# Graph-transformer kernel: in the edge pass VectorE weighs the value rows and sums the key products two quads at a time

## The chip, the cores and the metric

The kernel runs on one core of one Trainium2 chip. The time is the device time of one execution in microseconds; lower is better.

## The reference, cut to what matters

The program is a two-layer graph transformer over 3125 nodes with 256 features and 100,000 edges sorted by destination. What the change touches is the edge attention of the second layer (8 heads of 32 columns):

```python
scores = jnp.einsum('ehd,ehd->eh', q[dst], k[src] + ep[:, None, :]) * scale
scores = scores * ew[:, None]
m = jax.ops.segment_max(scores, dst, num_segments=n)
ex = jnp.exp(scores - m[dst])
s = jax.ops.segment_sum(ex, dst, num_segments=n)
attn = ex / s[dst]
out = jax.ops.segment_sum(attn[:, :, None] * v[src], dst, num_segments=n)
```

Everything is float32.

## The kernel before, in words

`stage_flash` is the edge pass. Edges are taken in sub-blocks of 128, one edge on each partition. 16 sub-blocks are a *window*, four sub-blocks a *quad* (`G` = 4 quads in a window). There are `NW` = 52 windows. For each sub-block GpSimd gathers 128 rows of 520 columns into a slot of a ring in SBUF: the key's 256 columns (`LO`) and 264 value columns (`HI_`, 33 a head, of which the last is a one that gives the sum of the weights). The ring has two sides of 16 slots.

Each engine runs the loop `windows`, whose `body(s, a, ffn)` does two windows at once: window `s` gets its scores, window `a`, the one before, is weighed and added up. The first call has only `s`, the last only `a`, 51 have both; 50 of these have `ffn` too, half a tile of another layer's feed-forward on TensorE and ScalarE.

For window `s`, quad by quad:

- TensorE, `ask(s, g)`: eight matmul instructions in the trace fetch the query rows of the quad's edges into `query`, a PSUM tile that holds one quad. It waits for `mult(s, g - 1)`, which frees that tile, and for the selection matrix `mem_t` from ScalarE.
- VectorE, `add(s, g)` (L2701): key rows plus edge features. `mult(s, g)` (L2708): times `query`, after `ask(s, g)`. `reduce(s, g)` (L2712): the sum over a head's 32 columns, into `dots`. After four quads `scale(s)` (L2718) makes the scores of the window.

For window `a`: TensorE transposes the scores (L2528), VectorE makes running maxima (`within`, `across`, `lower`) with small matmuls between them, ScalarE makes the exponentials `pa` (L2645). Then:

- VectorE, `rescale(a)` (L2768) on the row of `acc` that is carried on, and `weigh(a, g)` (L2773): the quad's value rows times their weights, which raises `pv_ready` by 1.
- TensorE, `collect(a, n)` (L2513) for sub-block pairs n = 0 to 7: sums of the value rows by destination. It waits for `pv_ready` of its quad, n // 2. `fold(a, n)` (L2520) adds the accumulator; ScalarE's `keep` (L2623) copies the sum back. A fold frees ring slots for GpSimd's next gathers.

Each engine works its queue strictly in the order of `body`; the order was written by hand. On TensorE it is: transpose of the scores, feed-forward, small matmuls, `ask(s, 0)`, small matmuls, feed-forward, `ask(s, 1)`, collects and folds of pairs 0 to 2, `ask(s, 2)`, pairs 3 and 4, `ask(s, 3)`, the rest. Semaphores count: `pv_ready` rises by `G` = 4 a window, and so do `mult_done` and `reduce_done`.

Of the kernel before, what the change touches and what calls it, by code (L numbers as in the profile page):

```python
# [18 lines left out]
ALU = mybir.AluOpType  # L19
# [3 lines left out]
P = 128  # L23
# [11 lines left out]
WS = 16  # L35
# [2271 lines left out]
def stage_flash(nc, sh, w1, w2, b1):  # L2307
# [6 lines left out]
    with ExitStack() as ctx:  # L2314
# [107 lines left out]
        with nc.Block() as block:  # L2422
# [246 lines left out]
            def _(dve):  # L2669
# [23 lines left out]
                def key_rows(s, g):  # L2693
                    return ring[:, s.side * WS + 4 * g:s.side * WS + 4 * g + 4, LO]
# [12 lines left out]
                    r = key_rows(s, g)  # L2707
                    dve.tensor_tensor(r, r, query[:, :].rearrange("p (k f) -> p k f", k=4), ALU.mult).then_inc(mult_done, 1)  # L2708

                def reduce(s, g):  # L2710
                    dve.wait_ge(mult_done, G * s.at + (g + 1))
                    dve.tensor_reduce(dots[:, g * 4 * H:(g + 1) * 4 * H].rearrange("p (k h) -> p k h", h=H),  # L2712
                                      key_rows(s, g).rearrange("p k (h d) -> p k h d", h=H), AX.X, ALU.add
                                      ).then_inc(reduce_done, 1)

                def scale(s):
                    dve.wait_ge(reduce_done, G * s.at + G)
# [49 lines left out]
                    r = sh.acc[:, bass.ds(tile, 1), :, :].rearrange("p a h v -> p (a h) v")  # L2767
                    dve.tensor_tensor(r, r, pa[:, P:P + H].unsqueeze(2).to_broadcast([P, H, VW]), ALU.mult).then_inc(rescaled, 1)  # L2768

                def weigh(a, g):  # L2770
                    r = ring[:, a.side * WS + 4 * g:a.side * WS + 4 * g + 4, HI_].rearrange("p k (h v) -> p k h v", h=H)
                    e = pa[:, 0:P].rearrange("p (h j) -> p j h", h=H)[:, 4 * g:4 * g + 4, :]
                    dve.tensor_tensor(r, r, e.unsqueeze(3).to_broadcast([P, 4, H, VW]), ALU.mult).then_inc(pv_ready, 1)  # L2773

                def body(s, a, ffn):
                    if a is not None and s is not None:
                        dve.tensor_copy(index[:, a.side * WS:(a.side + 1) * WS], sh.src_of[:, bass.ds(WS * s.at + WS, WS)]
                                        ).then_inc(index_ready, 1)
                    if s is not None:
                        add(s, 0)  # L2780
                    if a is not None:
                        within(a)
                        across(a)
                    if s is not None:
                        add(s, 1)
                    if a is not None:
                        lower(a)
                    if s is not None:
                        mult(s, 0)
                    if a is not None:  # L2790
                        tile = dve.value_load(sh.tile_id[0:1, bass.ds(WI * a.at, 1)], min_val=0, max_val=NT - 1)
                        rescale(a, tile)
                        weigh(a, 0)
                        weigh(a, 1)
                    if s is not None:
                        mult(s, 1)
                        add(s, 2)
                    if a is not None:
                        weigh(a, 2)
                    if s is not None:  # L2800
                        reduce(s, 0)
                        reduce(s, 1)
                        mult(s, 2)
                    if a is not None:
                        weigh(a, 3)
                    if s is not None:
                        add(s, 3)
                        reduce(s, 2)
                        mult(s, 3)
                        reduce(s, 3)  # L2810
                        scale(s)
                    if ffn is not None and ffn[1] == 1:
                        i = ffn[0]
                        dve.wait_ge(down_ready, 2 * i + 3)
                        w = sh.work[:, bass.ds(i, 1), :].rearrange("p a f -> p (a f)")
                        dve.tensor_tensor(w, w, down[:, 0:D], ALU.add).then_inc(down_added, 1)
# [415 lines left out]
```

## Time and profile before

| | |
|---|---|
| median of 3 runs | 4058.91 us (4058.58 to 4063.38) |
| span of the profiled execution, first to last instruction | 4057.2 us |
| VectorE busy | 2274.9 us (56%) |
| TensorE matmul busy | 3096.2 us (76%) |
| GpSimd busy | 1908.2 us (47%) |
| edge pass, from about 2215 to 3550 us of the span | about 1335 us |

The profile gives no other time of that execution than its span; the median of the runs is 1.7 us above it. In the views that follow, a row of the order of time is: start in us, duration in us (from the first start to the last end, where several are merged), engine, line, operation, what it writes and reads, count, and in brackets the idle time before it with what ended it. The end of one VectorE instruction can lie behind the start of the next, since the next one starts before the last results are written.

### The profile page before, as it was taken

The numbers are of one execution on the slowest core, as the hardware profiler recorded it, in microseconds if no ns is written. First come the engines' busy times: TensorE is split into PE (matmuls) and PEld (weight loads), VectorE is DVE, ScalarE is ACT, GpSimd is POOL, SyncE is SP. The second block draws the span as 40 slices with busy tenths as digits, with TensorE's granted clock in tenths as the row PEclk, the third lists the DMA queues.
The fourth block names the chain that finished last, engine by engine and source line by source line (L and its number), as shares of the span: only waits on it lengthen the run. The fifth ranks groups of instructions, "written<-read, shape, count | busy, mean of one in ns | idle before, by whom it ended". The sixth has DMA issues, their size and how long they took to land. (4 is left out here: it accounts for less than half of the span.)

```text
span 4057.2 us, 61852 instructions
## 1 busy us (share of the span) xinstructions
PE 3096.2 (76%) x13267; PEld 2402.7 (59%) x13268; DVE 2274.9 (56%) x5192; ACT 1703.0 (42%) x3865; POOL 1908.2 (47%) x1849
## 2 busy tenths in 40 slices
PE   2587777777767639906753899999999999849888
PEld 1476666666653438803332677777777777636655
DVE  6243333333345300043475899999999999762524
ACT  1333333333332112301402677777777777622413
POOL 2477777777760130040013666666666666420010
PEclk9677777778778569957876999999999999969999
DMA  5555555555540046623002777777777777510000
GB/s 145 160 150 144 145 143 142 143 143 144 143 97 0 14 141 205 204 67 123 32 0 90 223 217 215 216 216 216 213 215 217 218 217 217 157 39 22 1 24 32
DMA packets 347067, 552.91 MB, mean 136 GB/s; under 512 B 169831, under 2 KB 230771, under 8 KB 343109
## 3 DMA queue, kind: packets, MB, share of 16 engines
q0 software_dynamic: 114432, 353.45, 30.7%
q1 hardware_dynamic: 232305, 197.83, 17.0%
q10 hardware_dynamic: 260, 0.80, 0.1%
q8 instruction: 31, 0.51, 0.1%
q14 instruction: 39, 0.32, 0.0%
HBM read 489.26 MB, written 63.83 MB: 136 GB/s over the span
## 5 line engine op out<-in xcount | busy, mean ns | idle before, releaser
L2475 POOL DMA_INDIRECT store<-kv_d,flash_index x832 | 891.8, 1072 | 403.9 <-issue 227.9
L814 POOL DMA_INDIRECT agg_rows<-xn_d,agg_index x832 | 791.6, 951 | 321.9 <-issue 226.6
L839 ACT ACTIVATE agg_rows<-agg_rows,weight_of 128x256 f32<-128x256 f32 x832 | 368.5, 499 | 605.2 <-DMA agg_rows<-xn_d,agg_index 603.0
L989 PE MATMUL agg_sums<-agg_rows,agg_member 128*128 128x257 f32 x1664 | 515.5, 477 | 125.8 <-DVE agg_member L918 125.8
L989 PEld LDWEIGHTS agg_sums<-agg_rows,agg_member 128*128 128x128 f32 x1664 | 400.0, 247 | 223.3 <-ACT agg_rows L839 76.2
L925 DVE TENSOR_TENSOR acc<-acc,agg_sums 128x257 f32 x416 | 176.5, 424 | 589.6 <-PE agg_sums L989 507.3
L2500 PE MATMUL flash_query<-q,flash_mem_t 128*128 x1664 | 411.9, 391 | 50.6 <-DVE store L2708 38.7
L2513 PE MATMUL flash_sums<-store,flash_member 128*128 128x264 f32 x1664 | 423.0, 387 | 2.2 <-DVE store L2773 2.2
L2500 PEld LDWEIGHTS flash_query<-q,flash_mem_t 128*128 128x128 f32 x1664 | 313.2, 193 | 103.7 <-issue 63.1
L981 PE MATMUL agg_edge<-agg_we,agg_feats 65*128 65x32 f32 x1664 | 276.3, 336 | 114.0 <-DMA agg_feats<-in_ef_t_dram 113.9
L981 PEld LDWEIGHTS agg_edge<-agg_we,agg_feats 65*128 65x128 f32 x1664 | 271.9, 259 | 131.1 <-issue 130.3
L2513 PEld LDWEIGHTS flash_sums<-store,flash_member 128*128 128x128 f32 x1664 | 314.1, 191 | 59.2 <-issue 2.4
L2708 DVE TENSOR_TENSOR store<-store,flash_query 128x1024 f32<-128x1024 f32 x208 | 252.9, 1216 | 27.8 <-PE flash_query L2500 27.8
L2614 ACT ACTIVATE flash_member<-lane,lane_of 128x128 f32<-128x128 f32 x832 | 264.7, 395 | 0.0
L2520 PE MATMUL flash_sums<-acc,ident 128*128 x832 | 259.2, 393 | 1.5 <-ACT acc L2623 1.5
L2701 DVE TENSOR_TENSOR store<-store,flash_ep 128x1024 f32<-128x1024 f32 x208 | 253.1, 1217 | 8.9 <-DMA flash_ep<-ep_d 8.9
L2773 DVE TENSOR_TENSOR store<-store,flash_pa 128x1056 f32<-128x1056 f32 x208 | 256.1, 1253 | 0.0
L2623 ACT ACTIVATE acc<-flash_sums 128x264 f32 x416 | 159.3, 383 | 229.3 <-PE flash_sums L2520 222.8
L2712 DVE TENSOR_REDUCE flash_dots<-store 128x32 f32<-128x1024 f32 x208 | 248.3, 1216 | 1.8
L918 DVE TENSOR_SCALAR agg_member<-lane,lane_of 128x128 f32<-128x128 f32 x832 | 177.4, 303 | 34.8 <-issue 34.8
L1563 DVE COPY expert_y<-expert_down 128x512 f32<-128x512 f32 x32 | 22.1, 692 | 298.8 <-PE expert_down L1530 298.8
L2520 PEld LDWEIGHTS flash_sums<-acc,ident 128*128 128x128 f32 x832 | 145.6, 190 | 46.0 <-issue 30.6
(440 smaller groups left out, 4627.5 us busy)
## 6 DMA issues: line engine op xcount, KB each, us to landing
expert_w<-in_L_ffn_W_dram SPq DMA_DIRECT2D x64, 512.0 KB, 4.5
agg_feats<-in_ef_t_dram SPq DMA_DIRECT2D x52, 512.0 KB
flash_goal<-goal_d SPq DMA_DIRECT2D x52, 512.0 KB, 4.3
agg_rows<-xn_d,agg_index POOLq DMA_INDIRECT x832, 2.7
ep_d<-agg_ep SPq DMA_DIRECT2D x52, 256.0 KB
store<-kv_d,flash_index POOLq DMA_INDIRECT x832, 4.0
flash_ep<-ep_d SPq DMA_DIRECT2D x416, 32.0 KB
flash_flags<-flags_d SPq DMA_DIRECT2D x416, 32.0 KB
```

The costliest lines, as they stand in the source:

```text
L814: pool.indirect_dma_start(rows[:, q, 0:D], None, sh.xn_d, bass.IndirectOffsetOnAxis(ap=index[:, q:q + 1], axis=0)).then_inc(gathered[u], 16)
L839: act.activation(rows[:, q, 0:D], rows[:, q, 0:D], ACT.Copy, scale=sh.weight_of[:, bass.ds((UI * i + u) * SUBS + k, 1)]).then_inc(weighted, 1)
L981: last = pe.matmul(edge[:, c * DH:(c + 1) * DH], feats[:, c * P:(c + 1) * P], we_s[:, :], start=True, stop=True)
L989: last = pe.matmul(sums[:, u % 4, 0:W], member[:, u % WI * SUBS + k, :], rows[:, q, :], start=(k == 0), stop=(k == SUBS - 1))
L2475: pool.indirect_dma_start(ring[:, s, :], None, sh.kv_d, bass.IndirectOffsetOnAxis(ap=index[:, s:s + 1], axis=0)).then_inc(gathered[p][g], 16)
L2500: last = pe.matmul(query[:, c * D:(c + 1) * D], mem_t[:, g % 2, c * P:(c + 1) * P], sh.q[:, bass.ds(t, 1), :], start=True, stop=True)
L2513: pe.matmul(sums[:, n % 3, 0:W], member[:, g % 2, c, :], ring[:, a.side * WS + 4 * g + c, HI_], start=(k == 0), stop=False)
L2520: pe.matmul(sums[:, n % 3, 0:W], sh.ident[:, :], sh.acc[:, bass.ds(tiles[n], 1), :, :].rearrange("p a h v -> p (a h v)"), start=False, sto ...
L2614: act.activation(member[:, g % 2, k, :], sh.lane[:, :], ACT.Abs, scale=-1.0, bias=sh.lane_of[:, bass.ds(WS * a.at + (4 * g + k), 1)])
L2701: dve.tensor_tensor(r, r, ep[:, s.side, 4 * g:4 * g + 4, :].unsqueeze(2).to_broadcast([P, 4, H, DH]), ALU.add).then_inc(add_done, 1)
L2708: dve.tensor_tensor(r, r, query[:, :].rearrange("p (k f) -> p k f", k=4), ALU.mult).then_inc(mult_done, 1)
L2773: dve.tensor_tensor(r, r, e.unsqueeze(3).to_broadcast([P, 4, H, VW]), ALU.mult).then_inc(pv_ready, 1)
```

## The change

`weigh(a, g)` is replaced by `weigh_two(a, g)`: one instruction over 8 slots, which raises `pv_ready` by 2. `reduce(s, g)` is replaced by `reduce_two(s, g)`: one instruction over 8 slots, which waits for the `mult` of both quads and raises `reduce_done` by 2. `body` calls them in the order below.

```diff
-                def reduce(s, g):
-                    dve.wait_ge(mult_done, G * s.at + (g + 1))
-                    dve.tensor_reduce(dots[:, g * 4 * H:(g + 1) * 4 * H].rearrange("p (k h) -> p k h", h=H),
-                                      key_rows(s, g).rearrange("p k (h d) -> p k h d", h=H), AX.X, ALU.add
-                                      ).then_inc(reduce_done, 1)
+                def reduce_two(s, g):
+                    dve.wait_ge(mult_done, G * s.at + (g + 2))
+                    r = ring[:, s.side * WS + 4 * g:s.side * WS + 4 * g + 8, LO]
+                    dve.tensor_reduce(dots[:, g * 4 * H:(g + 2) * 4 * H].rearrange("p (k h) -> p k h", h=H),
+                                      r.rearrange("p k (h d) -> p k h d", h=H), AX.X, ALU.add).then_inc(reduce_done, 2)
...
-                def weigh(a, g):
-                    r = ring[:, a.side * WS + 4 * g:a.side * WS + 4 * g + 4, HI_].rearrange("p k (h v) -> p k h v", h=H)
-                    e = pa[:, 0:P].rearrange("p (h j) -> p j h", h=H)[:, 4 * g:4 * g + 4, :]
-                    dve.tensor_tensor(r, r, e.unsqueeze(3).to_broadcast([P, 4, H, VW]), ALU.mult).then_inc(pv_ready, 1)
+                def weigh_two(a, g):
+                    r = ring[:, a.side * WS + 4 * g:a.side * WS + 4 * g + 8, HI_].rearrange("p k (h v) -> p k h v", h=H)
+                    e = pa[:, 0:P].rearrange("p (h j) -> p j h", h=H)[:, 4 * g:4 * g + 8, :]
+                    dve.tensor_tensor(r, r, e.unsqueeze(3).to_broadcast([P, 8, H, VW]), ALU.mult).then_inc(pv_ready, 2)
...
                         rescale(a, tile)
-                        weigh(a, 0)
-                        weigh(a, 1)
+                        weigh_two(a, 0)
                     if s is not None:
                         mult(s, 1)
                         add(s, 2)
                     if a is not None:
-                        weigh(a, 2)
+                        weigh_two(a, 2)
                     if s is not None:
-                        reduce(s, 0)
-                        reduce(s, 1)
+                        reduce_two(s, 0)
                         mult(s, 2)
-                    if a is not None:
-                        weigh(a, 3)
-                    if s is not None:
                         add(s, 3)
-                        reduce(s, 2)
                         mult(s, 3)
-                        reduce(s, 3)
+                        reduce_two(s, 2)
                         scale(s)
```

VectorE's queue in the loop body, from the rescale of `acc` to the instruction before `mult(s, 2)` (L2708 is `mult`, L2701 `add`, L2773 `weigh` or `weigh_two`, L2712 `reduce`, L2713 `reduce_two`; `-` is before, `+` is now):

```order
 L2768 TENSOR_TENSOR acc<-acc,flash_pa 128x264
-L2773 TENSOR_TENSOR store<-store,flash_pa 128x4x264 x2
+L2773 TENSOR_TENSOR store<-store,flash_pa 128x8x264
 L2705 REGISTER_ALU
 L2708 TENSOR_TENSOR store<-store,flash_query 128x4x256
 L2701 TENSOR_TENSOR store<-store,flash_ep 128x4x256
-L2773 TENSOR_TENSOR store<-store,flash_pa 128x4x264
-L2712 TENSOR_REDUCE flash_dots<-store 128x32 x2
+L2773 TENSOR_TENSOR store<-store,flash_pa 128x8x264
+L2713 TENSOR_REDUCE flash_dots<-store 128x64
```

The first two quads are weighed by one instruction, and quad 3 has moved up in front of the sums of the key products.

The same queue from `mult(s, 2)` to `scale(s)`:

```order
 L2705 REGISTER_ALU
 L2708 TENSOR_TENSOR store<-store,flash_query 128x4x256
-L2773 TENSOR_TENSOR store<-store,flash_pa 128x4x264
-L2701 TENSOR_TENSOR store<-store,flash_ep 128x4x256
-L2712 TENSOR_REDUCE flash_dots<-store 128x32
+L2701 TENSOR_TENSOR store<-store,flash_ep 128x4x256
 L2705 REGISTER_ALU
 L2708 TENSOR_TENSOR store<-store,flash_query 128x4x256
-L2712 TENSOR_REDUCE flash_dots<-store 128x32
+L2713 TENSOR_REDUCE flash_dots<-store 128x64
 L2718 ISA
 L2718 SCALAR_TENSOR_TENSOR flash_scaled<-flash_dots,weight_of 128x16x8
```

Between `mult(s, 2)` and `mult(s, 3)` only `add(s, 3)` is left; the sum of quad 2 has moved behind `mult(s, 3)`. The queues of the other engines are the same as before.

## Rows read from the trace of the kernel before

**Rows 1.** The page: span, busy time of each engine, VectorE in 40 slices.
```profile
span 4057.2 us, 61852 instructions
...
PE 3096.2 (76%) x13267; PEld 2402.7 (59%) x13268; DVE 2274.9 (56%) x5192; ACT 1703.0 (42%) x3865; POOL 1908.2 (47%) x1849
...
DVE  6243333333345300043475899999999999762524
```
**Rows 2.** Stretches: length, busy PE, PEld, DVE, ACT, POOL (instructions); granted clock, DMA, GB/s.
```profile
2602.34:2627.00 24.66, 23.03 (x111) 18.69 (x111) 22.98 (x37) 18.09 (x42) 16.91 (x17) 1.00 0.74 212
2627.00:2652.13 25.13, 23.72 (x115) 19.23 (x115) 23.31 (x38) 17.50 (x42) 17.39 (x17) 1.00 0.76 221
```
**Rows 3.** Order of time on VectorE (DVE), one window from `mult(s, 0)` to `scale`.
```profile
2609.38 1.21 DVE L2708 TENSOR_TENSOR store<-store,flash_query 128x1024 f32<-128x1024 f32 x1
...
2611.07 2.42 DVE L2773 TENSOR_TENSOR store<-store,flash_pa 128x1056 f32<-128x1056 f32 x2
2613.41 1.22 DVE L2708 TENSOR_TENSOR store<-store,flash_query 128x1024 f32<-128x1024 f32 x1
...
2615.67 1.25 DVE L2773 TENSOR_TENSOR store<-store,flash_pa 128x1056 f32<-128x1056 f32 x1
2616.84 2.34 DVE L2712 TENSOR_REDUCE flash_dots<-store 128x32 f32<-128x1024 f32 x2
2619.59 1.22 DVE L2708 TENSOR_TENSOR store<-store,flash_query 128x1024 f32<-128x1024 f32 x1 [0.41 <-PE flash_query L2500]
...
2623.04 1.22 DVE L2712 TENSOR_REDUCE flash_dots<-store 128x32 f32<-128x1024 f32 x1
2624.16 1.21 DVE L2708 TENSOR_TENSOR store<-store,flash_query 128x1024 f32<-128x1024 f32 x1
2625.41 1.22 DVE L2712 TENSOR_REDUCE flash_dots<-store 128x32 f32<-128x1024 f32 x1
2626.78 0.37 DVE L2718 SCALAR_TENSOR_TENSOR flash_scaled<-flash_dots,weight_of 128x128 f32<-128x128 f32 x1
```
**Rows 4.** Order of time on TensorE (PE) in the same window.
```profile
2610.84 1.99 PE L2500 MATMUL flash_query<-q,flash_mem_t 128*128 x8 [0.68 <-DVE store L2708]
2612.67 1.05 PE L2513 MATMUL flash_sums<-store,flash_member 128*128 128x264 f32 x4
...
2617.60 1.89 PE L2500 MATMUL flash_query<-q,flash_mem_t 128*128 x8
...
2621.99 1.89 PE L2500 MATMUL flash_query<-q,flash_mem_t 128*128 x8
...
2626.42 0.64 PE L2520 MATMUL flash_sums<-acc,ident 128*128 x2
2627.21 0.33 PE L2528 MATMUL flash_small<-ident,flash_scaled 128*128 128x128 f32 x1
```
**Rows 5.** Order of time in the last window, which has only `a`.
```profile
3533.96 4.76 DVE L2773 TENSOR_TENSOR store<-store,flash_pa 128x1056 f32<-128x1056 f32 x4
...
3535.31 2.10 PE L2513 MATMUL flash_sums<-store,flash_member 128*128 128x264 f32 x4 [2.17 <-DVE store L2773]
```
**Rows 6.** Groups by form on VectorE, 2200 to 3400 us: busy, mean ns, idle before.
```profile
L2773 DVE TENSOR_TENSOR store<-store,flash_pa 128x1056 f32<-128x1056 f32 x184 | 226.7, 1253 | 0.0
...
L2768 DVE TENSOR_TENSOR acc<-acc,flash_pa 128x264 f32 x46 | 20.0, 434 | 5.6
```
**Rows 7.** Waits of VectorE in 36 windows (2602.34 to 3498.8): total, times, longest.
```profile
DVE store L2708 <- PE flash_query L2500: 14.9, 36, 0.4
```
**Rows 8.** Order of time on TensorE in the window without feed-forward, and that stretch.
```profile
3501.40 0.23 PE L2544 MATMUL flash_small<-flash_z,flash_row_head 128*8 128x32 f32 x2 [2.40 <-DVE flash_z L2733]
3501.61 3.67 PE L2500 MATMUL flash_query<-q,flash_mem_t 128*128 x8
...
3498.80:3526.20 27.40, 22.55 (x87) 17.63 (x88) 22.79 (x37) 14.45 (x35) 9.67 (x9) 0.88 0.37 99
```
**Rows 9.** Order of time on GpSimd (POOL): the first gather behind a wait.
```profile
2616.33 1.42 POOL L2475 DMA_INDIRECT store<-kv_d,flash_index  x1 [3.18 <-PE flash_sums L2520]
```

## Prediction

> **What bounds the kernel now.** I read the busy shares first. The edge pass is the stretch of slices in which VectorE's digit is 9: the pass keeps VectorE at nine tenths and more, while over the whole span it is busy for little over half [rows 1]. A window of 16 ring slots takes 24.66 and 25.13 us in turn; of these VectorE is busy 23.0 to 23.3 us and TensorE 23.0 to 23.7 us [rows 2]. Two engines at 93 to 95% can't be told apart by their shares, so I read the two engines' order of time inside one window, from `mult(s, 0)` at 2609.38 to `scale` at 2626.78, which is 17.40 us [rows 3, 4].
>
> In that stretch each engine waits for the other once. TensorE starts `ask(s, 1)` at 2610.84 after waiting 0.68 us for `mult(s, 0)` [rows 4]. From there on it runs one row behind the other: eight query matmuls, the `collect` and `fold` pairs, `ask(s, 2)` at 2617.60, more pairs, `ask(s, 3)` at 2621.99. VectorE waits 0.41 us for `ask(s, 2)`, and starts `mult(s, 2)` at 2619.59, 1.99 us behind that ask's start [rows 3, 4]. This isn't one odd window: in 36 windows VectorE's wait for the query comes 36 times and none is above 0.4 us, 14.9 us in all [rows 7]. So from `mult(s, 0)` to `mult(s, 2)` the path runs through TensorE, and from `mult(s, 2)` to `scale` through VectorE, which does seven instructions there without a gap. From `scale` to the next `mult(s, 0)` (24.9 - 17.4 = 7.5 us on average) VectorE is on the path again; the change touches nothing there.
>
> GpSimd isn't the bound: it waits 3.18 us for a `fold` that frees ring slots, and starts to gather at 2616.33 what VectorE adds to behind the next `scale` [rows 9]. A later `fold` delays the gathers by less than the window grows, below, so this cover stays.
>
> **What is in hand at mult(s, 3).** It starts at 2624.16, right behind `reduce(s, 2)` [rows 3]. By the 1.99 us just read, `ask(s, 3)`, which starts at 2621.99, would have let it start at 2623.98. So the slack of TensorE's path is only 0.18 us at this point, and what VectorE does between `mult(s, 2)` and `mult(s, 3)` was hidden time for TensorE almost to the last tenth.
>
> **The change, part by part.** Per window, four `weigh` become two of double size and four `reduce` become two.
>
> *Price of a double instruction.* A `weigh` of 1056 elements takes 1253 ns, the rescale (the same kind of operation) of 264 elements 434 ns [rows 6]: 819 / 792 = 1.034 ns an element. The second half of a double `weigh` adds 1056 x 1.034 = 1.09 us; of a double `reduce`, 1024 x 1.034 = 1.06, up to the 1.13 us that lies between starts of 1024-element instructions that don't depend on each other (two of them fill 2613.41 to 2615.67) [rows 3]. I take 1.07. The instruction saved is worth start distance less streaming time: 1.17 - 1.09 = 0.08 us for a `weigh`, 1.13 - 1.07 = 0.06 for a `reduce`, so 2 x 0.08 + 2 x 0.06 = 0.28 us of VectorE's work a window.
>
> *Step 1, the first collect.* `collect(a, 0)` needs quad 0 alone, but its semaphore now moves when quads 0 and 1 are both weighed. Before, quad 0 was ready at 2611.07 + 1.25 = 2612.32, hidden behind `ask(s, 1)`; the collect started at 2612.67 when TensorE came free. Now both are ready at 2611.07 + 1.25 + 1.09 = 2613.41. How fast TensorE follows is seen where it did wait for a `weigh`: the last window, the first of four starts at 3533.96 and ends 1.25 us later, at 3535.21, and TensorE starts at 3535.31, 0.10 us [rows 5]. The nearest rows on both sides are 0.06 us (`scale`'s end, 2627.15, to the transpose at 2627.21) and 0.25 us (`mult(s, 0)`'s end, 2610.59, to the ask at 2610.84) [rows 3, 4]. I take 0.10: the collect starts at 2613.51, 0.84 us late (0.80 to 0.99). Behind it stand the whole of TensorE's queue: all collects and folds, `ask(s, 2)`, `ask(s, 3)`. ScalarE's copies of the sums wait for the folds and move along with them. TensorE has no gap until `ask(s, 3)` in which to catch up [rows 4], so all of it is 0.84 us late.
>
> *Step 2, quad 3 weighed earlier.* `weigh_two(a, 2)` puts 1.09 us more in front of `mult(s, 2)`. VectorE would have been ready for that at 2619.18; now at about 2619.18 + 1.09 - 0.14 = 2620.1. The query comes at 2619.59 + 0.84 = 2620.43. Hidden by step 1's delay; without step 1 it would cost about 0.5 us at `mult(s, 2)`, though not at `mult(s, 3)`, since there is 1.17 us less behind it.
>
> *Step 3, what stood between mult(s, 2) and mult(s, 3).* `weigh(a, 3)` and `reduce(s, 2)` are gone from there, `add(s, 3)` alone is left. That can't bring `mult(s, 3)` forward, since its query isn't there: `ask(s, 3)` starts at 2621.99 + 0.84 and lets it start at 2624.82, 0.66 us later than before. VectorE is ready at about 2620.43 + 1.13 + 1.25 = 2622.8 and stands idle for 2.0 us.
>
> *Step 4, the last reduce.* Behind `mult(s, 3)` there was one quad to sum, now there are two: +1.07 us (1.06 to 1.13) until `scale`. `reduce(s, 2)`, which ran in time that TensorE needed anyway, now runs in time that everybody waits for: the transpose at 2627.21 begins right behind `scale` [rows 3, 4], and the whole chain to the next `mult(s, 0)` hangs on it.
>
> The sum for a window: 0.84 - 0.18 + 1.07 = 1.73 us; by the bounds 0.80 - 0.18 + 1.06 = 1.68 to 0.99 - 0.18 + 1.13 = 1.94. Windows that do both halves of the work: 51. The first window (scores only) has step 4 alone, +1.07; the last (weighing only) step 1 alone, +1.09. Together 51 x 1.73 + 2.2 = 90 us, with bounds of 88 and 101. The span becomes 4057.2 + 90.4 = 4147.6 us; the median of the runs is 1.7 us above the profiled span, so 4149 us, with 4147 to 4160 from the bounds.
>
> The 0.28 us of saved work is all inside the 2.0 us of new idle time, so it is worth nothing. The Trainium skill ("VectorE: DVE Perf Modes", the section on the TRN2 errata, and "Rules for kernel authors") says the opposite of this forecast: every SBUF instruction pays a fixed latency once, so few large ones are better, and one should minimize the number of operations. The trace agrees on the fixed cost (0.06 to 0.08 us an instruction) but not on its being on the path.
>
> **The rivals.**
> *The count decides (faster).* VectorE is the bound at 93%, so less work is less time: -0.28 x 51 = -14 us, 4045 us. For it speaks only the busy share. It needs TensorE to be off the path between `mult(s, 0)` and `mult(s, 3)`: it would decide if TensorE's stretch from 2610.84 to 2623.98 were shorter by over 1.7 us (0.84 + 1.07 - 0.18), which the 0.41 us wait excludes.
> *The shifts cancel (no change).* TensorE's late start is absorbed by its own waits elsewhere and the moved `weigh` gives `mult(s, 3)` what step 4 takes: 4059 us. Against it stands the 0.18 us.
> *One delay alone.* TensorE makes up its late start before `ask(s, 3)`, because its ends are modelled and it isn't as full as it seems. Then step 4 stays: 1.07 - 0.18 = 0.89 a window, 51 x 0.89 + 2 = 47 us, 4106 us.
> *TensorE's clock falls (slower still).* TensorE now idles about 0.7 us before the first collect (2610.84 + 1.99 = 2612.83 to 2613.51) and about 1 us before the transpose (the last fold ends at 2626.42 + 0.64 + 0.84 = 2627.90, `scale` at 2627.15 + 1.73), and 1.6 + 1.7 = 3.3 us of a 26.6 us window in all [rows 2, 4]. In the last full window, which has no feed-forward matmuls, it waited 2.40 us and its next eight query matmuls took 3.67 us in place of 1.89 to 1.99: the granted clock had gone to the lower level, 1.2 GHz [rows 8]. That window took 27.4 us (3498.80 to 3526.20), 2.6 more than a usual one. If every window did so, 51 x 2.6 = 133 us on top: about 4280 us. Against it: the new idle stretches are each shorter than 2.40 us, with 2 us of matmuls between them.
>
> **How the numbers follow.** Forecast 0.77; one delay alone 0.10; clock 0.05; cancel 0.04; count 0.04. The forecast's own range is 4142 to 4164 us (the bounds, and 4 us either way for what the windows differ by). That leaves 0.23 out, so the range goes down to the single delay: 4104 to 4164. A change of 0.2%, 8 us, is about what can be told from none. Faster 0.04, the same 0.04, slower 0.92.
>
> **What would show it.** Right: a full window of 26.4 to 26.8 us; VectorE waiting for the query some 2.0 us before `mult(s, 3)` and 0.3 us before `mult(s, 2)`; TensorE waiting for the double `weigh` before the first collect, once a window; double instructions of 2.28 to 2.35 us; the transpose about 19.5 us behind `mult(s, 0)` in place of 17.8; TensorE's clock at full. Wrong: the first collect still behind the ask at once (step 1), `mult(s, 3)` at the old distance of 14.8 us from `mult(s, 0)` (step 3), a double instruction priced other than 1.07 to 1.13 us above a single one (step 4), query matmuls of over 3 us per ask (clock), or a window of under 24.7 us (count).

## The result: 110 us slower, and the profile after

On the same chip, with four runs of each, the changed kernel takes 4169.81 us (4161.95 to 4173.39) and the kernel before 4059.57 us (4058.58 to 4063.38). The ratio is 1.0267, 95% interval 1.0252 to 1.0281: slower. The forecast was 4149 us with a range up to 4164: the time lies 6 us above the range. Direction and mechanism held, and the size of the loss was forecast too small.

The page of after: span, busy time of each engine, VectorE in 40 slices.

```profile
span 4160.3 us, 61748 instructions
...
PE 3107.1 (75%) x13267; PEld 2398.4 (58%) x13268; DVE 2267.8 (55%) x4984; ACT 1705.8 (41%) x3865; POOL 1871.2 (45%) x1849
...
DVE  5243333333445200143576888888888888862524
```

VectorE issues 208 instructions fewer (5192 to 4984, four in each of 52 windows) and is busy 7.1 us less, while the span is 103.1 us longer [rows 1]. Its digit in the edge pass fell from 9 to 8: the engine that looked like the bound now has idle time.

Two groups by form on VectorE, 2200 to 3500 us (busy, mean ns of one, idle before), answer to [rows 6]:

```profile
L2773 DVE TENSOR_TENSOR store<-store,flash_pa 128x2112 f32<-128x2112 f32 x92 | 216.3, 2351 | 0.0
L2713 DVE TENSOR_REDUCE flash_dots<-store 128x64 f32<-128x2048 f32 x94 | 214.5, 2282 | 4.8
```

A double `weigh` is 2351 - 1253 = 1098 ns above a single one. The price of a double instruction was right (1.09 forecast, and 2.28 to 2.35 us for the whole).

The waits of after between 2200 and 3560 us (total, times, longest) answer to [rows 7]:

```profile
DVE store L2708 <- PE flash_query L2500: 130.2, 98, 3.9
...
PE flash_sums L2513 <- DVE store L2773: 40.5, 49, 0.8
```

Before, VectorE waited for the query once a window, 0.4 us each. Now it waits twice a window, 98 times, and TensorE has a wait that it didn't have: 0.83 us for the double `weigh`, once a window.

Order of time on VectorE in one window of after, from `mult(s, 0)` to `scale`; it answers to [rows 3]:

```profile
2608.47 1.22 DVE L2708 TENSOR_TENSOR store<-store,flash_query 128x1024 f32<-128x1024 f32 x1
...
2610.15 2.35 DVE L2773 TENSOR_TENSOR store<-store,flash_pa 128x2112 f32<-128x2112 f32 x1
...
2619.77 1.22 DVE L2708 TENSOR_TENSOR store<-store,flash_query 128x1024 f32<-128x1024 f32 x1 [0.54 <-PE flash_query L2500]
2620.91 1.22 DVE L2701 TENSOR_TENSOR store<-store,flash_ep 128x1024 f32<-128x1024 f32 x1
2624.17 1.22 DVE L2708 TENSOR_TENSOR store<-store,flash_query 128x1024 f32<-128x1024 f32 x1 [2.04 <-PE flash_query L2500]
2625.49 2.29 DVE L2713 TENSOR_REDUCE flash_dots<-store 128x64 f32<-128x2048 f32 x1
2627.92 0.38 DVE L2718 SCALAR_TENSOR_TENSOR flash_scaled<-flash_dots,weight_of 128x128 f32<-128x128 f32 x1
```

And on TensorE in the same window; it answers to [rows 4]:

```profile
2609.93 1.99 PE L2500 MATMUL flash_query<-q,flash_mem_t 128*128 x8 [0.68 <-DVE store L2708]
2612.74 1.15 PE L2513 MATMUL flash_sums<-store,flash_member 128*128 128x264 f32 x4 [0.83 <-DVE store L2773]
2613.73 0.61 PE L2520 MATMUL flash_sums<-acc,ident 128*128 x2
...
2617.78 1.89 PE L2500 MATMUL flash_query<-q,flash_mem_t 128*128 x8
...
2622.17 1.89 PE L2500 MATMUL flash_query<-q,flash_mem_t 128*128 x8
...
2628.36 0.33 PE L2528 MATMUL flash_small<-ident,flash_scaled 128*128 128x128 f32 x1 [1.11 <-DVE flash_scaled L2718]
```

To compare the two kernels I measure every instruction from `mult(s, 0)` of its window. Medians over the 51 full windows, in us:

| behind `mult(s, 0)` | before | after |
|---|---|---|
| first `collect` | 3.29 | 4.27 |
| `mult(s, 2)` | 10.21 | 11.31 |
| `ask(s, 3)` | 12.61 | 13.70 |
| `mult(s, 3)` | 14.79 | 15.70 |
| `scale(s)` | 17.40 | 19.46 |
| from `scale` to the next `mult(s, 0)` | 7.8 | 7.8 |

(The rows of `collect` and `ask(s, 3)` are from the windows shown in [rows 3, 4] and above.) Nearly all the loss lies between `mult(s, 0)` and `scale`: 2.06 us. Over the pass, the first `scale` to the 52nd goes from 2251.8 to 3526.2 us before and from 2248.9 to 3629.8 after: 24.99 and 27.08 us a window, 51 x 2.09 = 106.5 us. Outside this stretch the span is 3.4 us shorter, which gives the 103.1. The profiled run was the shortest of the four of after; the medians differ by 110.

### The profile page after: what moved, and what is told of

Its sections match the earlier page's. It is cut to its first block and busy times, and to the rows that moved or that the text cites. A ratio compares the mean times of both kernels' runs of the same rounds, so it can differ in the third digit from the quotient of the medians.

```text
span 4160.3 us, 61748 instructions
## 1 busy us (share of the span) xinstructions
PE 3107.1 (75%) x13267; PEld 2398.4 (58%) x13268; DVE 2267.8 (55%) x4984; ACT 1705.8 (41%) x3865; POOL 1871.2 (45%) x1849
## 5 line engine op out<-in xcount | busy, mean ns | idle before, releaser
L2475 POOL DMA_INDIRECT store<-kv_d,flash_index x832 | 854.8, 1027 | 545.3 <-PE flash_sums L2520 302.6
L2708 DVE TENSOR_TENSOR store<-store,flash_query 128x1024 f32<-128x1024 f32 x208 | 253.2, 1217 | 138.4 <-PE flash_query L2500 138.4
L2701 DVE TENSOR_TENSOR store<-store,flash_ep 128x1024 f32<-128x1024 f32 x208 | 253.7, 1220 | 9.2 <-DMA flash_ep<-ep_d 8.2
L2773 DVE TENSOR_TENSOR store<-store,flash_pa 128x2112 f32<-128x2112 f32 x104 | 244.4, 2351 | 0.0
L2713 DVE TENSOR_REDUCE flash_dots<-store 128x64 f32<-128x2048 f32 x104 | 237.3, 2282 | 5.4
```

The costliest lines, as they stand in the source:

```text
L2475: pool.indirect_dma_start(ring[:, s, :], None, sh.kv_d, bass.IndirectOffsetOnAxis(ap=index[:, s:s + 1], axis=0)).then_inc(gathered[p][g], 16)
L2701: dve.tensor_tensor(r, r, ep[:, s.side, 4 * g:4 * g + 4, :].unsqueeze(2).to_broadcast([P, 4, H, DH]), ALU.add).then_inc(add_done, 1)
L2773: dve.tensor_tensor(r, r, e.unsqueeze(3).to_broadcast([P, 8, H, VW]), ALU.mult).then_inc(pv_ready, 2)
```

## The experiments

**How they are read.** The runs `v0` and `v5` were on a chip on which the kernel before takes 4060 us, as in the result. All others were on five other chips, on which the kernel before takes 4777 to 4828 us. I call these the slow chips. On them every kernel has additional stalls, in the edge pass and before it. In the views of waits, `remote` is a release by something that isn't an instruction of this core's profile, and `issue` is time in which the engine waited for nothing that the profile shows. The waits of the kernel before on such a chip, between 2500 and 3560 us:

```profile
ACT acc L2623 <- remote: 198.1, 50, 6.7
PEld flash_sums L2520 <- issue: 171.5, 90, 5.9
...
DVE store L2708 <- remote: 58.3, 23, 9.6
```

A window takes 33.8 us there in place of 25.0. The durations of instructions at full clock are the same, and some windows have no stall between `mult(s, 0)` and `scale`: I call them undisturbed. In the list of distances of all 51 windows they are the shortest. There are one to eleven of them in each run, only one in `z0`, `x2`, `y2`, `w7`, `u1` and `u3`; within a kernel they agree to 0.05 us. So on these chips the order of time inside undisturbed windows tests the theory, and the total only tells what a kernel does amid the stalls.

TensorE's clock is lower there too. Between 2600 and 4200 us the granted clock (the number ahead of the DMA share, columns as in [rows 2]) is 0.89 for the kernel before (`z0`), 0.89 for the changed one (`z5`) and 0.86 for one that comes below (`z3`), where the pass on the fast chip has 1.00:

```profile
2600.00:4200.00 1600.00, 1245.74 (x5293) 999.21 (x5293) 1104.02 (x1723) 841.34 (x1955) 773.37 (x759) 0.89 0.56 159
...
2600.00:4200.00 1600.00, 1223.02 (x5181) 972.38 (x5181) 1071.08 (x1499) 825.08 (x1920) 759.46 (x743) 0.89 0.55 156
...
2600.00:4200.00 1600.00, 1224.26 (x5110) 970.31 (x5111) 1059.50 (x1577) 816.33 (x1903) 812.39 (x731) 0.86 0.55 153
```

**The kernels of the result again.** `z0` is the kernel before and `z5` the changed one, unaltered, on one slow chip.

> The kernel before, unchanged, for its trace. If this chip is like that of the x and y runs: some 4780 us and, once a window, a stall of 4 to 6 us on all engines that no semaphore explains, as in x1 to x4, so that the stalls belong to the chip and not to the experiments. If the stalls come with the edits: 4059 us and none of them.

> The changed kernel, unchanged, beside the kernel before on this chip. Where VectorE isn't disturbed, scale 19.46 us behind mult(s, 0). On a chip without the stalls +108 us, a ratio of 1.027. On a chip with them the ratio is smaller if the stalls cover part of the two delays, and 1.022 (108 / 4780) if they only add.

Measured: `z0` 4789.53 us beside 4787.62 in the other runs of before; its undisturbed window has `mult(s, 3)` at 14.79 and `scale` at 17.40. `z5` 4830.48 us, ratio 1.0084 (1.0056 to 1.0113); four undisturbed windows with 15.70 and 19.45. Both patterns are those of the fast chip to 0.01 us, so the reading by undisturbed windows holds. The price in total is about a third of that on the fast chip: the time from `scale` to the next `mult(s, 0)`, summed over the 50 gaps between full windows, is 697 us for `z0` and 652 for `z5` (377 and 380 on the fast chip). So the gain there, 45 us, takes back part of what the longer windows cost; I read it as stalls that were there anyway and that the later `scale` covers.

**Undo step 1** (the steps are those of the prediction; step 1 is the first collect). The changed kernel with the first double `weigh` as two single ones:

```diff
-                        weigh_two(a, 0)
+                        weigh(a, 0)
+                        weigh(a, 1)
```

> The changed kernel with its first double weigh split again into weigh(a, 0) and weigh(a, 1); the double reduces and the double weigh of quads 2 and 3 stay. Two delays in series: the first collect is no longer late (2.05 less 1.10 us a window), mult(s, 3) comes 0.18 us earlier than in the kernel before, and the doubled last reduce costs 1.13, so +0.95 us a window over before, about 4059 + 49 = 4108 us. If the long reduce alone made the loss: no gain over the changed kernel, 4168. If the late collect alone made it: 4059.

Order of time on VectorE in an undisturbed window:

```profile
3146.33 1.22 DVE L2708 TENSOR_TENSOR store<-store,flash_query 128x1024 f32<-128x1024 f32 x1
...
3148.01 2.42 DVE L2773 TENSOR_TENSOR store<-store,flash_pa 128x1056 f32<-128x1056 f32 x2
...
3160.94 1.22 DVE L2708 TENSOR_TENSOR store<-store,flash_query 128x1024 f32<-128x1024 f32 x1 [1.51 <-PE flash_query L2500]
...
3164.70 0.37 DVE L2718 SCALAR_TENSOR_TENSOR flash_scaled<-flash_dots,weight_of 128x128 f32<-128x128 f32 x1
```

On TensorE in the same window:

```profile
3147.79 1.99 PE L2500 MATMUL flash_query<-q,flash_mem_t 128*128 x8 [0.68 <-DVE store L2708]
3149.61 1.05 PE L2513 MATMUL flash_sums<-store,flash_member 128*128 128x264 f32 x4
```

The first collect is behind the ask at once, `mult(s, 3)` comes at 14.61 and `scale` at 18.37 (six windows agree; `y1` on another chip gives 18.36 in eight, `u1` on a third 18.36 in one). That is 0.97 us over the kernel before, 0.95 expected. Step 1 costs 19.46 - 18.37 = 1.09 us. And 14.61 against 14.79 is the slack: once quad 3's `weigh` and quad 2's `reduce` are out of the way, `mult(s, 3)` starts when its query comes, 0.18 us earlier, just what [rows 3, 4] gave. `mult(s, 2)` is at 10.75 here, 0.54 later than before: step 2's price without its cover, and it doesn't reach `mult(s, 3)`.

**Undo step 4.** The changed kernel with `reduce(s, 2)` ahead of `mult(s, 3)` again:

```diff
-                        mult(s, 3)
-                        reduce_two(s, 2)
+                        reduce(s, 2)
+                        mult(s, 3)
+                        reduce(s, 3)
```

> The changed kernel with its last double reduce split again: reduce(s, 2), mult(s, 3), reduce(s, 3); both double weighs and the first double reduce stay. Two delays in series: the first collect is 1.08 us late, mult(s, 3) 0.91 us late, and the last reduce is one quad as before: +0.91 us a window, 4059 + 46 = 4105 us. If the long reduce alone made the loss: 4059. If the late collect alone made it: 4168.

Measured: `mult(s, 3)` at 15.73 and `scale` at 18.35 in the undisturbed window (`y2`: 15.75 and 18.38). Step 4 (the sum of quad 2 behind `mult(s, 3)`) costs 1.1 us, in the stretch behind `mult(s, 3)`: 2.62 us to `scale`, as before, against 3.76 in the changed kernel.

**Undo both.** The two edits above together; two double instructions are left, the second `weigh` and the first `reduce`.

> Both of these at once: single weighs of quads 0 and 1, single reduces of quads 2 and 3; what is left of the change is the double weigh of quads 2 and 3 in front of the sums, and the double reduce of quads 0 and 1. By the path: nothing late on TensorE, mult(s, 2) about 0.5 us late and hidden, mult(s, 3) 0.18 us earlier since only add and reduce stand before it: -0.18 us a window, 4059 - 9 = 4050 us. If the moved weigh in front of mult(s, 2) is on the path: +0.5 us a window, 4084. If fewer instructions alone count: no other than 4059 within 8.

An undisturbed window, on VectorE:

```profile
2792.28 1.21 DVE L2708 TENSOR_TENSOR store<-store,flash_query 128x1024 f32<-128x1024 f32 x1
...
2806.89 1.22 DVE L2708 TENSOR_TENSOR store<-store,flash_query 128x1024 f32<-128x1024 f32 x1 [0.38 <-issue]
...
2809.51 0.37 DVE L2724 SCALAR_TENSOR_TENSOR flash_scaled<-flash_dots,weight_of 128x128 f32<-128x128 f32 x1
```

`scale` is at 17.23, that is 0.17 us less than before, in seven windows (17.22 to 17.23 in the undisturbed windows of `y3`, `z3`, `w3` and `u3`). The two delays are the whole loss of the undisturbed window, and what is left of the change gains the slack. The total doesn't follow, see below.

**Order without fusion.** The changed order with eight single instructions in the places of the four double ones:

```diff
-                        weigh_two(a, 2)
+                        weigh(a, 2)
+                        weigh(a, 3)
...
-                        reduce_two(s, 2)
+                        reduce(s, 2)
+                        reduce(s, 3)
```

(and the first of each likewise).

> No double instruction at all, only the changed kernel's order on VectorE: quads 2 and 3 weighed in front of the reduces of quads 0 and 1, and reduce(s, 2) moved behind mult(s, 3). By the path: no late collect; mult(s, 3) at 14.60 us behind mult(s, 0); reduce(s, 2) needs only mult(s, 2), so it starts 1.13 behind mult(s, 3) and not 1.25, and scale comes at 14.60 + 1.13 + 1.13 + 1.37 = 18.23 (before 17.40, with the double reduce 18.36). +0.83 us a window, 4101 us on a chip without the stalls. If the size of the instructions makes the loss and not their place: 17.40 or less, 4059.

Its undisturbed window, on VectorE:

```profile
2555.58 1.21 DVE L2708 TENSOR_TENSOR store<-store,flash_query 128x1024 f32<-128x1024 f32 x1
...
2570.19 1.22 DVE L2708 TENSOR_TENSOR store<-store,flash_query 128x1024 f32<-128x1024 f32 x1 [1.38 <-PE flash_query L2500]
2571.32 2.34 DVE L2712 TENSOR_REDUCE flash_dots<-store 128x32 f32<-128x1024 f32 x2
2573.81 0.37 DVE L2724 SCALAR_TENSOR_TENSOR flash_scaled<-flash_dots,weight_of 128x128 f32<-128x128 f32 x1
```

18.23, in its one undisturbed window. Against `x3` (`mult(s, 3)` is at 14.61 in both), putting quad 2's sum behind `mult(s, 3)` costs 1.00 us; against `x1`, making one instruction of the last two costs another 0.14 us. The rows show why. The single `reduce(s, 2)` doesn't need `mult(s, 3)` and starts 1.13 us behind its start (2571.32); the double one does need it and starts 1.32 us behind (2625.49 - 2624.17), which is more than the 0.06 us that fusing saves.

The window's loss now adds up from the runs: 17.40 to 17.23 (the slack), 18.23 (order of the sums), 18.37 (their fusion), 19.46 (the first `weigh` signals late).

**A late signal alone.** The kernel before, in which the first `weigh` doesn't signal and the second signals for both:

```diff
-                        weigh(a, 0)
-                        weigh(a, 1)
+                        weigh(a, 0, 0)
+                        weigh(a, 1, 2)
```

(the last argument is by how much `pv_ready` rises).

> The kernel before with one edit: weigh(a, 0) gives no signal and weigh(a, 1) gives both. All instructions, their sizes and their order are those of the kernel before, only the first collect's wait ends later. By the path: first collect 1.06 us late (weigh(a, 1) ends at 2613.49, plus 0.24), 0.10 more for starting from a stand, less the 0.18 in hand: mult(s, 3) and scale +0.98 us a window, 4059 + 50 = 4109 us on a chip without the stalls. If it is the size of the instructions that costs: no change, 4059.

An undisturbed window, on VectorE:

```profile
2716.43 1.21 DVE L2708 TENSOR_TENSOR store<-store,flash_query 128x1024 f32<-128x1024 f32 x1
...
2718.12 2.42 DVE L2773 TENSOR_TENSOR store<-store,flash_pa 128x1056 f32<-128x1056 f32 x2
...
2727.80 1.22 DVE L2708 TENSOR_TENSOR store<-store,flash_query 128x1024 f32<-128x1024 f32 x1 [1.57 <-PE flash_query L2500]
...
2734.98 0.38 DVE L2718 SCALAR_TENSOR_TENSOR flash_scaled<-flash_dots,weight_of 128x128 f32<-128x128 f32 x1
```

On TensorE in the same window:

```profile
2720.77 1.15 PE L2513 MATMUL flash_sums<-store,flash_member 128*128 128x264 f32 x4 [0.90 <-DVE store L2773]
2721.76 0.61 PE L2520 MATMUL flash_sums<-acc,ident 128*128 x2
```

`scale` is at 18.55, 1.15 us late (0.98 expected), in four undisturbed windows. No instruction of VectorE differs from the kernel before; the signal alone does it. This is the cause of step 1 by itself. It also shows what I had missed in the size: the collect starts 2720.77 - 2718.12 - 2.42 = 0.23 us behind the end of the `weigh`, not 0.10, and its four matmuls take 1.15 us, not 1.05. Here all of it reaches `scale`, since VectorE has no idle time between `mult(s, 2)` and `mult(s, 3)` in this order; the expectation had wrongly taken off the 0.18 us of slack.

**What lies between the signal and the matmul.** In the changed kernel, `collect` waits for `member_ready`, then `pv_ready`, then `added` (the first two pairs only). `x4` puts `added` first:

```diff
-                    pe.wait_ge(member_ready, G * a.at + (g + 1))
-                    pe.wait_ge(pv_ready, G * a.at + (g + 1))
                     if n < 2:
                         pe.wait_ge(added, WI * a.at + (n + 1))
+                    pe.wait_ge(member_ready, G * a.at + (g + 1))
+                    pe.wait_ge(pv_ready, G * a.at + (g + 1))
```

> The changed kernel with the three waits of collect in another order on TensorE: `added` first, `member_ready` and `pv_ready` last, so that no register instruction stands between the wait for the weigh and the matmul. If that register instruction is what made the first collect start 0.24 us behind the weigh's end and not 0.10: the lag falls to about 0.10, -0.14 us a window, -7 us against the changed kernel, about 4161 us. If the 0.24 us is how long TensorE takes whenever it has stood idle: no change.

An undisturbed window, on VectorE:

```profile
3480.58 1.21 DVE L2708 TENSOR_TENSOR store<-store,flash_query 128x1024 f32<-128x1024 f32 x1
...
3482.27 2.35 DVE L2773 TENSOR_TENSOR store<-store,flash_pa 128x2112 f32<-128x2112 f32 x1
...
3499.92 0.37 DVE L2718 SCALAR_TENSOR_TENSOR flash_scaled<-flash_dots,weight_of 128x128 f32<-128x128 f32 x1
```

On TensorE in the same window:

```profile
3484.77 1.13 PE L2513 MATMUL flash_sums<-store,flash_member 128*128 128x264 f32 x4 [0.74 <-DVE store L2773]
```

The collect starts 0.15 us behind the end of the `weigh` (49 windows within 0.01) in place of 0.24, and `scale` is at 19.34 (`y4` the same) in place of 19.45. Only the order of three waits differs. The expectation was a lag of 0.10, so two thirds of it came. In the changed kernel's trace the last of the three, L2510, is a line with instructions of its own in the queue of TensorE's weight loads (count; min/median/max ns; first and last start):

```profile
L2510 PEldq EVENT_SEMAPHORE  x54: 51/51/3560, 2261.8 to 3640.4; - x54
L2510 PEldq ALU_OP  x50: 32/32/32, 2261.4 to 3586.1; - x50
```

Of these only the `ALU_OP` stands in front of the first collect. In the changed kernel's window shown further up, the wait for `pv_ready` (L2508, 51 ns) is in the queue at 2612.5, right behind the end of the `weigh`, the `ALU_OP` at 2612.7 and the first weight load at 2612.74; the `EVENT_SEMAPHORE` of L2510 comes at 2613.0, for the second pair. With the waits reordered, the weight load (3484.74) follows the wait for `pv_ready` (3484.7) directly. In the last window neither of the two instructions stands there, and the lag is 0.10.

**A suspect for the stalls.** The load of `goal` (512 KB a window) was left out from the third window on, in the kernel before (`v0`) and in the changed one (`v5`), so that from there on the queries are picked by the destinations of earlier windows:

```diff
-                    if not first:
-                        sp.wait_ge(off_ready, G * w - G)
-                    sp.dma_start(goal[:, p, :], ...).then_inc(goal_in[p], 16)
+                    if first:
+                        sp.dma_start(goal[:, p, :], ...).then_inc(goal_in[p], 16)
...
-                        act.wait_ge(goal_in[s.side], 16 * s.turn)
+                        act.wait_ge(goal_in[s.side], 16)
```

> The kernel before without the load of `goal` from the third window on (the selection matrices are then those of the first two windows, so the attention sums are not those of the reference): 512 KB a window, one row written to 128 partitions. On four chips a window took 34 to 35 us in place of 25.0, with stalls of 2 to 5 us on all engines that begin some 5 us behind this load's issue. If the load makes them: windows of about 25 us and a span some 400 us shorter than the kernel before on this chip. If another transfer or the chip as a whole makes them: windows of 33 to 34 us still.

> The changed kernel with the same load left out (same consequence for the output). If the stalls are gone with it: the two delays in series show in the total, 2.05 us a window more than v0, 107 us in all. If the stalls stay: 40 to 50 us more than v0, as z5 to its kernel before.

These two landed on a chip without the stalls, so they tell nothing of them. They do tell that the load costs nothing there (`v0` 4059.82 us beside 4059.78 of before, ratio 1.0002, 0.9991 to 1.0013), and they measure the change a second time: `v5` 4166.02 us, ratio 1.0259 (1.023 to 1.0289), 27.07 us a window, `scale` at 19.45.

**Repeats on other chips.** Steps 1 and 4 undone, alone and together, and the reordered waits were run again:

> The same kernel as x1_single_first_weighs. Two delays in series: the first collect no longer late, the doubled last reduce stays, +0.95 us a window over before, 4108 us. Long reduce alone: 4168. Late collect alone: 4059.

> The same kernel as x2_single_last_reduces. Two delays in series: the collect 1.08 us late, mult(s, 3) 0.91 us late, one quad in the last reduce, +0.91 us a window, 4105 us. Long reduce alone: 4059. Late collect alone: 4168.

> The same kernel as x3_both_single, on another chip if there is one: in the x runs every kernel, the one before too, took some 700 us more, with stalls of 4 to 6 us a window on all engines that no semaphore explains, so they tell nothing of 1 us a window. Single weighs of quads 0 and 1, single reduces of quads 2 and 3. By the path: -0.18 us a window against the kernel before, 4050 us; mult(s, 3) 14.6 us behind mult(s, 0). If the moved weigh in front of mult(s, 2) counts: 4084.

> The same kernel as x4_pv_wait_last: `added` waited for first, `member_ready` and `pv_ready` last. If the register instruction between the wait and the matmul makes the lag: first collect 0.10 us behind the weigh's end in place of 0.24, -7 us against the changed kernel, 4161 us. If TensorE takes 0.24 us whenever it has stood idle: 4168.

> Single weighs of quads 0 and 1, single reduces of quads 2 and 3; left of the change: the double weigh of quads 2 and 3, in front of the double reduce of quads 0 and 1. On a chip without the stalls: -0.18 us a window, 4050 us. On one with them: as x3 and y3, 1.012 to 1.013 times the kernel before, though the undisturbed windows are 0.17 us shorter, since something else than this path decides there.

> Single weighs of quads 0 and 1, single reduces of quads 2 and 3, double weigh of quads 2 and 3 moved up, double reduce of quads 0 and 1. In undisturbed windows of x3, y3 and z3 scale came 17.23 behind mult(s, 0), as against 17.40. On a chip without the stalls of several us a window: 0.17 x 51 = 9 us less than the kernel before, 4050 us. On one with them as before, 1.012 to 1.013 times the kernel before.

> Only the late first collect undone. On a chip without the stalls: scale 18.36 behind mult(s, 0), +0.96 us a window and 1 us for the first window, 4060 + 50 = 4110 us. If the moved reduce were hidden in the total: 4060; if the late collect were: 4168.

> Both delays undone (single weighs of quads 0 and 1, single reduces of quads 2 and 3), the rest of the change kept. If the chip is one without the stalls: -0.17 us a window against the kernel before, 4060 - 9 = 4051 us. If something else than the two delays is in the loss: above 4060.

In the undisturbed windows each came out within 0.04 us of its first run, as given above. The totals, which stand in the table below, missed: no kernel with both steps undone came below the kernel before, and with one step undone the ratio was 1.0129 to 1.0252 where 4105 to 4110 us against 4059, some 1.012, was expected. Of the expectations for a slow chip, `z3` met 1.012 to 1.013 and `w3`, at 1.0159, didn't.

**Totals on the slow chips.**

| kernel | median, ratio to before on its chip (95%) |
|---|---|
| changed (`z5`) | 4830.48, 1.0084 (1.0056 to 1.0113) |
| late signal alone (`z6`) | 4836.02, 1.0081 (1.0055 to 1.0107) |
| waits reordered (`x4`, `y4`) | 4824.56, 1.0107 (1.0074 to 1.0140); 4838.75, 1.0105 (1.0066 to 1.0143) |
| step 4 undone (`x2`, `y2`) | 4860.75, 1.0166 (1.0136 to 1.0197); 4835.61, 1.0129 (1.0082 to 1.0177) |
| step 1 undone (`x1`, `y1`, `u1`) | 4859.14, 1.0163 (1.0133 to 1.0193); 4868.31, 1.0186 (1.0148 to 1.0224); 4956.24, 1.0252 (1.0201 to 1.0302) |
| both undone (`x3`, `y3`, `z3`, `w3`, `u3`) | 4841.12, 1.0130 (1.0106 to 1.0155); the others 1.0123 to 1.0203 |
| order alone (`w7`) | 4863.15, 1.0177 (1.0160 to 1.0194) |

The totals don't follow the window: with both steps undone the undisturbed window is the shortest of all, and the total is over 1% above before. On one chip, the total of `z3` (both undone, 1.0123) is even above that of `z5` (the changed kernel, 1.0084). The time from `scale` to the next `mult(s, 0)` sums to 801 us in `x3`, 784 in `x1` and 782 in `w7`, against 697 in the kernel before and 652 in the changed one. One wait shows the place, between 2600 and 3900 us of `x1`:

```profile
DVE flash_run L2738 <- remote: 267.6, 32, 10.1
```

VectorE stands 32 times for 8.4 us in front of `run` in `x1` and 33 times in `w7` (271.8 us); in the kernel before on such a chip it is 65.0 us, 11 times, in the same stretch, and the stalls mostly fall on other instructions. ScalarE stands in the same place: in front of `hidden` (L2638) for 296.6 us, 35 times, in `x1`, and 49.2 us, 10 times, in `z0`. TensorE's clock goes with it only in part: 0.88 in `x1` and `w7`, 0.86 in `x3` and `z3`, 0.89 in `z0`. Why a kernel whose window is shorter meets longer stalls, and what the stalls are, stays open. So it stays open whether the version with both steps undone gains its 51 x 0.17 = 9 us on the fast chip: all five of its runs came on chips with stalls, and there it was 1.2 to 2.0% slower than the kernel before.

## Where the prediction was right, and which step failed

The step that failed is step 1, in the size of its delay: 0.84 us forecast, 1.09 measured. Two terms were wrong in it, the lag behind the `weigh` (0.10 taken, 0.24 measured) and the slower collect behind a wait (nothing taken, 0.10 measured). In step 4, 0.07 us was missing.

- **What bounds the kernel: right.** Two engines at 93 to 95% were told apart by their order of time, and TensorE's stretch from `ask(s, 1)` to `ask(s, 3)` carried its delay through as forecast. VectorE's saved work went into idle time: of 0.28 us a window nothing was gained. The rule cited from the Trainium skill ("VectorE: DVE Perf Modes", "Rules for kernel authors") is true of the engine's own time here, 7.1 us less busy, and didn't carry over to the kernel's, 103.1 us longer.
- **Step 1, mechanism right, mis-sized.** Forecast 0.84 us late; the collect came 0.98 late, and its four matmuls took 0.10 longer than in [rows 4], so `ask(s, 3)` was 13.70 - 12.61 = 1.09 late. Two terms failed. The lag behind the `weigh` was 0.24 us, not the 0.10 read from [rows 5]; the upper bound, 0.25 from `mult(s, 0)`'s end to the ask, was the right row. The last window is a poor model of the loop: it stands behind the loop, and `a.at` is a constant there. In the changed kernel's own last window the lag is again 0.10, as the rows below show; in the loop a register instruction for the wait on `added` stands in between, and `x4` took 0.09 us of the lag away by moving it. The 0.05 that is left beside 0.10 is as long as the separate wait for `pv_ready` (51 ns), which the last window doesn't have; no run took that one away. The second term, a slower collect after standing idle, was not in the sum at all. [rows 4] had shown it: the ask that starts after a wait takes 1.99 us, the two that start without one 1.89. The rows of the weight loads, below, show where the 0.10 lies.
- **The slack: right.** 0.18 us forecast, 0.18 measured in `x1` and `x3`.
- **Step 2: right.** Hidden, and 0.54 us at `mult(s, 2)` alone where its cover is gone (0.5 forecast).
- **Step 3: right.** `mult(s, 3)` waits 2.04 us for its query (2.0 forecast). The wait ahead of `mult(s, 2)` is 0.54, not 0.3, by the 0.25 us of step 1.
- **Step 4: nearly right.** From `reduce` to `scale` 2627.92 - 2625.49 = 2.43 us against 1.37 before: +1.06 (1.07 forecast). But the double `reduce` starts 1.32 us behind `mult(s, 3)` where the single one started 1.25 behind, 0.07 us that I had not counted.
- **The sum.** 1.09 - 0.18 + 0.07 + 1.06 = 2.04 us a window, by the medians 2.06; forecast 1.73, bounds 1.68 to 1.94. The missing 0.33 x 51 = 17 us, 13 of them from step 1 (0.25 x 51), cover the 12.7 us by which the span missed (103.1 longer, 90.4 forecast; outside the pass it is 3.4 us shorter). The upper bound, 4160, was too low too, since it held the right lag but neither the slower restart nor the later `reduce`. The rest of the 21 us between forecast and median is that the profiled run (4161.95) was 7.9 us below the median of its kernel; no trace shows what made the other three 6 to 11 us longer.
- **The rivals.** The clock stayed at full: two halves of the pass are shown below, both at 1.00. One delay alone, no change, and the count fall by the table of distances.

The weight loads (PEld) of the first collect, before and after, in the windows of [rows 4] and of the rows above:

```profile
2612.55 0.75 PEld L2513 LDWEIGHTS flash_sums<-store,flash_member 128*128 128x128 f32 x4
...
2612.74 0.74 PEld L2513 LDWEIGHTS flash_sums<-store,flash_member 128*128 128x128 f32 x4 [1.22 <-issue]
```

Before, the first load began 0.12 us ahead of the first matmul (2612.67), while the query matmuls still ran; after, load and matmul begin together at 2612.74, and, one instruction at a time, the second matmul starts 0.32 us behind the first in place of 0.22. So the 0.10 lies between the first two matmuls. That the cause is the first load, which nothing hides any more, fits these rows, but no run tests it.

The last window of after, on VectorE:

```profile
3637.66 4.62 DVE L2773 TENSOR_TENSOR store<-store,flash_pa 128x2112 f32<-128x2112 f32 x2
```

On TensorE in the same window:

```profile
3640.11 2.10 PE L2513 MATMUL flash_sums<-store,flash_member 128*128 128x264 f32 x4 [3.27 <-DVE store L2773]
```

The collect starts 3640.11 - 3637.66 = 2.45 us, less the 2.35 of one double `weigh`, leaves 0.10.

The pass in two stretches (columns as in [rows 2]); the granted clock is the number ahead of the DMA share:

```profile
2250.00:2935.00 685.00, 601.11 (x2842) 480.21 (x2841) 583.05 (x834) 449.87 (x1051) 414.96 (x404) 1.00 0.68 198
2935.00:3620.00 685.00, 597.98 (x2806) 477.32 (x2805) 582.82 (x818) 448.91 (x1044) 411.23 (x400) 1.00 0.67 196
```

## What to carry to other kernels

Fusing two instructions also fuses their signals and their waits. Before counting the fixed cost that is saved (0.06 to 0.08 us here), ask who waits for the first half and what the second half waits for: here the first consumer came 1.0 us later, and work that had stood in time which another engine needed anyway was put behind the last operand that arrives. It follows, though no fast-chip run here tests it, that fusing is safe only where nobody waits for the first half and both halves have their operands in hand.

A lag from one engine to another is to be read in the same code as the place in question, with the same waits between, and not in a copy of it outside the loop.

## What the runs showed of the hardware that I had not expected

- The lag from the end of a VectorE instruction to the matmul that waits for it was 0.24 us where the register instruction of another wait (32 ns) stood in between, 0.15 us with the waits reordered, and 0.10 us where the counts were constants.
- Groups of matmuls that start after a wait took longer here: four of `collect` 1.15 us against 1.05, eight of `ask` 1.99 against 1.89, the clock being 1.00. (`ask(s, 0)` takes 1.99 us too, behind two small matmuls that had waited.)
- Chips differ: the same kernel takes 4060 us on one and 4777 to 4828 on five others, with the same durations of instructions at full clock but stalls of several microseconds in most windows and a granted clock of 0.85 to 0.90 in the pass in place of 1.00. A change that costs 2.6% on the first cost 0.8% on one of the others, and on that one a kernel whose undisturbed window is 2.2 us shorter than the changed one's cost more than it did (1.2%).
